# All eight experts' weights resident on chip, addressed by a register

## What is computed

```
logits = x1n @ router_w.T                      # 4096 tokens, 8 experts
top_w, top_i = top_k(softmax(logits), 2)       # two experts per token
h = gelu(x1n @ w1[e])      # w1: 8 x 256 x 1024
y = h @ w2[e]              # w2: 8 x 1024 x 256
out = x1 + sum over the two experts of weight * y
```

## Time and profile before

| what | value |
|---|---|
| median of 3 runs | 728.38 us |
| the three runs | 718.8, 728.38, 732.76 us |
| span of the profiled execution (first to last instruction) | 716.1 us |
| the profiled execution's own time | not listed apart; the runs above lie 2.7 to 16.7 us over its span |
| PE busy | 616.2 us, 86% |
| DVE, ACT, POOL busy | 402.2, 299.7, 256.9 us |
| DMA | 130.52 MB, 182 GB/s mean |

### The profile page before, as it was taken

One profiled execution on the slowest core, in us unless ns is written; L12 is line 12 of the kernel. 1 busy time (PEld: TensorE's weight loads), 2 busy tenths in 40 slices (PEclk: granted clock), 3 DMA queues, 4 the chain that ended last, 5 costly groups with the idle time before them and its releaser, 6 DMA issues.

```text
span 716.1 us, 18339 instructions
## 1 busy us (share of the span) xinstructions
PE 616.2 (86%) x5879; PEld 498.6 (70%) x5879; DVE 402.2 (56%) x1118; ACT 299.7 (42%) x582; POOL 256.9 (36%) x192
## 2 busy tenths in 40 slices
PE   2799988988999830099999999999999999999991
PEld 2578777776887730078787777777787878777880
DVE  1458678687686655045555555555555555555550
ACT  2444634625444200044545444444544454544440
POOL 0213148568475467012133232233231322312322
PEclk9965657557565555599999999999999999999996
DMA  9786486594541425913944938537649358377321
GB/s 313 272 323 224 173 292 223 208 329 176 196 185 75 177 81 178 367 26 54 343 101 102 349 48 260 179 59 222 218 74 369 56 135 298 52 205 243 48 36 22
DMA packets 58964, 130.52 MB, mean 182 GB/s; under 512 B 6384, under 2 KB 38384, under 8 KB 57904
## 3 DMA queue, kind: packets, MB, share of 16 engines
q1 hardware_dynamic: 44384, 110.91, 43.2%
q0 software_dynamic: 13392, 18.10, 14.1%
q10 hardware_dynamic: 1152, 1.07, 0.4%
HBM read 188.49 MB, written 40.13 MB: 319 GB/s over the span
## 4 chain that ended last, share of the span: by engine, by line
PE 69%; DVE 8%; ACT 6%; issue 5%; DMA 5%; POOL 4%; SPq 2%; POOLq 0%; DVEq 0%; ACTq 0%
PE bank L664 16%; PE bank L650 9%; PE bank L652 9%; PE bank L651 9%; PE bank L666 8%; PE bank L542 6%; PE bank L485 5%; DMA out<-ct,dst 2%; PE bank L634 2%; PE bank L527 2%; POOL rows L1282 2%; ACT xn L695 2%; DMA xrow<-rows 1%; POOL hrs L1274 1%; DVE rowb L874 1%
## 5 line engine op out<-in xcount | busy, mean ns | idle before, releaser
L650 PE MATMUL bank<-dt,wring 128*128 128x128 f16 x1136 | 198.5, 220 | 1.1 <-DVE dt L1201 1.1
L652 PE MATMUL bank<-dt,wring 128*128 128x128 f16 x1136 | 198.6, 220 | 0.0
L651 PE MATMUL bank<-dt,wring 128*128 128x128 f16 x1136 | 198.5, 220 | 0.0
L664 PE MATMUL bank<-wring,ct 128*128 128x512 f16 x568 | 192.3, 379 | 1.3 <-DVE ct L1217 1.3
L1217 DVE TENSOR_TENSOR ct<-dt,ct 128x512 f16<-128x512 f32 x142 | 98.3, 692 | 139.0 <-PE bank L666 113.1
L814 ACT ACTIVATE dt<-bank 128x512 f32<-128x512 f32 x142 | 84.8, 597 | 216.3 <-PE bank L652 216.3
L666 PE MATMUL bank<-wring,ct 128*128 128x256 f16 x568 | 154.8, 273 | 0.0
L1318 POOL DMA_INDIRECT out<-ct,dst x48 | 76.6, 1596 | 211.8 <-DMA out<-ct,dst 75.8
L650 PEld LDWEIGHTS bank<-dt,wring 128*128 128x128 f16 x1136 | 111.3, 98 | 25.1 <-issue 15.7
L651 PEld LDWEIGHTS bank<-dt,wring 128*128 128x128 f16 x1136 | 111.4, 98 | 0.9
L652 PEld LDWEIGHTS bank<-dt,wring 128*128 128x128 f16 x1136 | 111.4, 98 | 0.0
(11 more groups left out here) (139 smaller groups left out, 830.2 us busy)
## 6 DMA issues: line engine op xcount, KB each, us to landing
wring<-wsplit SPq DMA_DIRECT2D x284, 512.0 KB
wring<-in_w SPq DMA_DIRECT2D x16, 1024.0 KB, 12.0
xrow<-rows SPq DMA_DIRECT2D x71, 130.0 KB
wsplit<-wring SPq DMA_DIRECT2D x4, 2048.0 KB, 8.4
wsplit<-wcv SPq DMA_DIRECT2D x4, 2048.0 KB, 7.9
xa<-in_x SPq DMA_DIRECT2D x8, 512.0 KB, 9.1
kT<-in_ctx_t SPq DMA_DIRECT2D x8, 512.0 KB, 8.6
ctn<-in_ctx SPq DMA_DIRECT2D x8, 512.0 KB, 8.4
```

The source lines that it names most:

```text
L650: pe.matmul(o, hi, xT[k][:, c, :], start=(c == 0), stop=False)
L651: pe.matmul(o, hi, xT[k][:, CK + c, :], start=False, stop=False)
L652: mm = pe.matmul(o, lo, xT[k][:, c, :], start=False, stop=(c == CK - 1))
L664: pe.matmul(YP[k][:, 0:2 * D], gh[a][:, m4, :], wring[:, k, w:w + 2 * D], start=(a == 0 and m4 == 0), stop=False, skip_group_check=True)
```

## The change

All eight experts' split weights get a place in one tensor `wall` of 128 KB in each partition, at the expert's number. The buffers of the attention stage (`xa`, `kT`, `ctn`) now lie in the places of experts 4 to 7, and the staging buffers of the weight split in those of 0 to 3. A tile's weights are loaded only where its expert differs from that of the tile just before, and SP works five tiles ahead instead of two (with a wait for the stored attention results, since their buffer is overwritten). The place is no longer known when the program is written, so SP's destination and every weight operand of PE is addressed by a register: PE loads the tile's expert from the table, and `weights(e, at, n)` names the slice.

```diff
-        xa = sb("xa", [P, NB, D])
-        kT = [sb(f"kT{p}", [P, G, CK, P]) for p in range(3)]
-        ctn = [sb(f"ctn{p}", [P, G, D]) for p in range(2)]
+        wall = sb("wall", [P, NE, 2 * (W1 + W2)], F16)
+        early = wall[:, NE // 2:NE, :].bitcast(F32).rearrange("p e n -> p (e n)")
+        xa = early[:, 0:NB * D].rearrange("p (b d) -> p b d", d=D)
...
-        wring = sb("wring", [P, RING, 2 * (W1 + W2)], F16)
-        wst = [wring[:, p, :].bitcast(F32) for p in range(2)]
-        wcv1 = sb("wcv1", [P, 2 * (W1 + W2)], F16)
-        wcv = [wring[:, 2, :], wcv1[:, :]]
+        wst = [wall[:, p, :].bitcast(F32) for p in range(2)]
+        wcv = [wall[:, 2 + p, :] for p in range(2)]
...
-            def load_weights(i, k, it):
+            def load_weights(i, o, it):
                 e = sp.value_load(tab[0:1, 0, bass.ds(i, 1)], min_val=0, max_val=NE - 1)
                 need = sp.value_load(tab[0:1, 2, bass.ds(i, 1)], min_val=0, max_val=1)
                 w_e = wsplit[bass.ds(e, 1)].rearrange("o p n -> (o p) n")
+                place = wall[:, bass.ds(e, 1), :].rearrange("p o n -> p (o n)")
                 for half, s_free, s_loaded in ((0, s_h, s_wr1), (1, s_m2, s_wr2)):
-                    after(sp, s_free, 2 * (i - RING + 1))
+                    after(sp, s_free, 2 * (i - OUT + 1))
...
-                        sp.dma_start(wring[:, k, at], w_e[:, at], cond=need).then_inc(s_loaded[k], 16)
+                        sp.dma_start(place[:, at], w_e[:, at], cond=need).then_inc(s_loaded[o], 16)
             def tile(i, k, o, it):
                 load_rows(i, k, it)
-                if not (isinstance(i, int) and i < RING):
-                    load_weights(i, k, it)
+                if not (isinstance(i, int) and i >= TILES - OUT + RING):
+                    j = o + OUT - RING
+                    load_weights(i + OUT - RING, j % OUT, it + j // OUT)
             sp.wait_ge(s_tab, 1)
+            sp.wait_ge(s_x1o, 16 * NG)
...
-                        hi = wring[:, k, c * HID + m * P:c * HID + (m + 1) * P]
-                        lo = wring[:, k, W1 + c * HID + m * P:W1 + c * HID + (m + 1) * P]
+                        hi = weights(e, c * HID + m * P, P)
+                        lo = weights(e, W1 + c * HID + m * P, P)
...
-                    pe.matmul(YP[k][:, 0:2 * D], gh[a][:, m4, :], wring[:, k, w:w + 2 * D],
+                    pe.matmul(YP[k][:, 0:2 * D], gh[a][:, m4, :], weights(e, w, 2 * D),
...
+            def expert(i):
+                return pe.value_load(tab[0:1, 0, bass.ds(i, 1)], min_val=0, max_val=NE - 1)
+            def weights(e, at, n):
+                return wall[:, bass.ds(e, 1), at:at + n].rearrange("p o n -> p (o n)")
             def tile(i, k, o, it):
-                hidden(i, k, it, 0)
+                e = expert(i)
+                hidden(i, k, o, it, e, 0)
                 if not (isinstance(i, int) and i == 0):
-                    output(i - 1, (k - 1) % RING, it, 1)
+                    output(i - 1, (k - 1) % RING, (o - 1) % OUT, it, expert(i - 1), 1)
-                hidden(i, k, it, 1)
+                hidden(i, k, o, it, e, 1)
...
-            link(dve.memset(chg[:, 0:RING], 1.0))
-            link(dve.tensor_tensor(chg[:, RING:TILES], etab[:, RING:TILES], etab[:, 0:TILES - RING], ALU.not_equal))
+            link(dve.memset(chg[:, 0:1], 1.0))
+            link(dve.tensor_tensor(chg[:, 1:TILES], etab[:, 1:TILES], etab[:, 0:TILES - 1], ALU.not_equal))
```

More of the change, by code:

```diff
@@ L116, in build @@
         mhalf = sb("mhalf", [P, R])
-        xa = sb("xa", [P, NB, D])
-        kT = [sb(f"kT{p}", [P, G, CK, P]) for p in range(3)]
-        ctn = [sb(f"ctn{p}", [P, G, D]) for p in range(2)]
+        wall = sb("wall", [P, NE, 2 * (W1 + W2)], F16)
+        early = wall[:, NE // 2:NE, :].bitcast(F32).rearrange("p e n -> p (e n)")
+        xa = early[:, 0:NB * D].rearrange("p (b d) -> p b d", d=D)
+        kT = [early[:, NB * D + p * G * D:NB * D + (p + 1) * G * D].rearrange("p (b j n) -> p b j n", b=G, j=CK)
+              for p in range(3)]
+        ctn = [early[:, NB * D + (3 + p) * G * D:NB * D + (4 + p) * G * D].rearrange("p (b d) -> p b d", b=G)
+               for p in range(2)]
         vt = [sb(f"vt{p}", [P, G, NH, DH + 1]) for p in range(2)]
@@ L306, in build @@
         s_xr = [sem(f"tile_loaded{i}") for i in range(RING)]
-        s_wr1 = [sem(f"tile_first_weights{i}") for i in range(RING)]
-        s_wr2 = [sem(f"tile_second_weights{i}") for i in range(RING)]
+        s_wr1 = [sem(f"tile_first_weights{i}") for i in range(OUT)]
+        s_wr2 = [sem(f"tile_second_weights{i}") for i in range(OUT)]
         s_xtp = sem("tile_transposed")
@@ L337, in spot @@
             def spot(j, it):
-                return OUT * it + j, j % RING, j, OUT // RING * it + j // RING
+                return OUT * it + j, j % RING, j, it
             for j in range(OUT):
@@ L346, in tiles, with it_rows @@
                 tile(*spot(j, TILES // OUT))
+        def it_rows(o, it):
+            return OUT // RING * it + o // RING
         block = stack.enter_context(nc.Block())
@@ L635, in turn, with hidden @@
                 mm.then_inc(s_xtp, 1)
-            def hidden(i, k, it, a):
+            def hidden(i, k, o, it, e, a):
                 if a == 0:
-                    pe.wait_ge(s_wr1[k], 16 * PIECES * (it + 1))
+                    pe.wait_ge(s_wr1[o], 16 * PIECES * (it + 1))
                     pe.wait_ge(s_xtc, i + 1)
@@ L645, in hidden, with output @@
                     m = 4 * a + m4
-                    o = HPS[a][:, m4 * P:(m4 + 1) * P]
+                    h = HPS[a][:, m4 * P:(m4 + 1) * P]
                     for c in range(CK):
-                        hi = wring[:, k, c * HID + m * P:c * HID + (m + 1) * P]
-                        lo = wring[:, k, W1 + c * HID + m * P:W1 + c * HID + (m + 1) * P]
-                        pe.matmul(o, hi, xT[k][:, c, :], start=(c == 0), stop=False)
-                        pe.matmul(o, hi, xT[k][:, CK + c, :], start=False, stop=False)
-                        mm = pe.matmul(o, lo, xT[k][:, c, :], start=False, stop=(c == CK - 1))
+                        hi = weights(e, c * HID + m * P, P)
+                        lo = weights(e, W1 + c * HID + m * P, P)
+                        pe.matmul(h, hi, xT[k][:, c, :], start=(c == 0), stop=False)
+                        pe.matmul(h, hi, xT[k][:, CK + c, :], start=False, stop=False)
+                        mm = pe.matmul(h, lo, xT[k][:, c, :], start=False, stop=(c == CK - 1))
                 mm.then_inc(s_h, 1)
-            def output(i, k, it, a):
+            def output(i, k, o, it, e, a):
                 if a == 0:
-                    pe.wait_ge(s_wr2[k], 16 * PIECES * (it + 1))
+                    pe.wait_ge(s_wr2[o], 16 * PIECES * (it + 1))
                 pe.wait_ge(s_gh, 2 * i + a + 1)
@@ L663, in output @@
                     w = 2 * W1 + (4 * a + m4) * 2 * D
-                    pe.matmul(YP[k][:, 0:2 * D], gh[a][:, m4, :], wring[:, k, w:w + 2 * D],
+                    pe.matmul(YP[k][:, 0:2 * D], gh[a][:, m4, :], weights(e, w, 2 * D),
                               start=(a == 0 and m4 == 0), stop=False, skip_group_check=True)
-                    mm = pe.matmul(YP[k][:, D:2 * D], gl[a][:, m4, :], wring[:, k, w:w + D],
+                    mm = pe.matmul(YP[k][:, D:2 * D], gl[a][:, m4, :], weights(e, w, D),
                                    start=False, stop=(a == 1 and m4 == 3), skip_group_check=True)
                 mm.then_inc(s_m2, 1)
+            def expert(i):
+                return pe.value_load(tab[0:1, 0, bass.ds(i, 1)], min_val=0, max_val=NE - 1)
+            def weights(e, at, n):
+                return wall[:, bass.ds(e, 1), at:at + n].rearrange("p o n -> p (o n)")
             def tile(i, k, o, it):
-                hidden(i, k, it, 0)
+                e = expert(i)
+                hidden(i, k, o, it, e, 0)
                 if not (isinstance(i, int) and i == 0):
-                    output(i - 1, (k - 1) % RING, it, 1)
-                hidden(i, k, it, 1)
+                    output(i - 1, (k - 1) % RING, (o - 1) % OUT, it, expert(i - 1), 1)
+                hidden(i, k, o, it, e, 1)
                 if not (isinstance(i, int) and i == TILES - 1):
-                    turn(i + 1, (k + 1) % RING, it + (k + 1) // RING)
-                output(i, k, it, 0)
+                    turn(i + 1, (k + 1) % RING, it_rows(o + 1, it))
+                output(i, k, o, it, e, 0)
             pe.wait_ge(s_sa, NG)
+            pe.wait_ge(s_tab, 1)
             turn(0, 0, 0)
             tiles(pe, tile)
-            output(TILES - 1, (TILES - 1) % RING, 0, 1)
+            output(TILES - 1, (TILES - 1) % RING, (TILES - 1) % OUT, 0, expert(TILES - 1), 1)
         @block.scalar
```

2 lines of the change are left out of this document (1 added, 1 removed).

## The result

| | before | after |
|---|---|---|
| median of three runs | 728.38 us | 857.34 us (857.19, 857.34, 858.57) |
| ratio after / before | | 1.185 [1.171, 1.199]: slower |
| span of the profiled execution | 716.1 us | 855.3 us |
| a tile (once-a-tile line of DVE) | 5.547 us | 7.586 us |
| table ready | 280.5 us | 289.5 us |

What follows compares the result with a forecast made beforehand. PE's sequencer was to replace PE's matmul stream as bound: 71 x (6.8 - 5.55) = +89 us, with -7.7 at the start and -5.7 at the end, gives a 792 us span, plus 12.3 is 804 us; range 755 to 1180.

Steps and rivals of the forecast that it cites:

- rival A: PE's sequencer: only control instructions cost, the forecast's own case, 804 us, own range 762 to 861; chance 0.50.
- the sum: PE's sequencer time a tile: 10 x 0.10 + 1.3 + 4.0 + 132 x 0.004 = 6.8 us, against 5.55 of matmuls.
- The start: Start of the expert stage: first rows land at 295.2 instead of 302.9, behind fewer weight loads: -7.7 us.
- the end: End of the expert stage: POOL's last scatter catches up with a third of the weight loads: -5.7 us.
- the price of an address: PE's sequencer: 40 fused register operations a tile at 0.10 us each, 4.0 us; bounds 1.3 to 6.3 us.
- Rival C: PE's register work runs beside the queued matmuls, so only the edges count: 715 us, -1.8%; chance 0.14.
- The offset of 12.3 us: Added to the forecast span of 792 us to give the median of the runs, 804 us.
- the first L634 near 295 us: Sign expected in any case at the start of the expert stage: the first L634 comes near 295 us.
- Triples: Sign for A in the hidden layer: matmul triples about 0.2 us apart instead of 0.167.
- Rival B: PE's 64 register-addressed weight loads or matmuls cost 0.032 to 0.10 us each: 946 to 1258 us; chance 0.29.
- Rival D: PE pauses often enough to be granted 1.2 GHz, 11.1 us a tile: about 1110 us; chance 0.07.
- Rival E: Tile order makes weights reload more often, so edges lose some of their 13 us; no chance of its own.

Runs made afterwards that it cites:

- one-slice kernel: Changed kernel with every hidden weight load taking the same slice, still addressed by register (9 address operations a tile instead of 40): one run of 717.14 us beside 726.73.
- fixed-address kernel: Changed kernel with PE back on fixed addresses and without its two register loads a tile: 707.4 us against 730.35 for the kernel before, ratio 0.971.

## Why the prediction was right in its direction and short in its size

**What held.** The time, 857.34 us, lies inside the range of 755 to 1180 and 53 us above the 804 named. The sequencer became the bound (rival A), by the steps named: 40 addresses and two loads a tile, counted in the rows; the clock at 1.00; 33.5 MB less. A load costs 0.63 us (forecast 0.65), or 0.67 in the five tiles of six that lose one. The rest of the tile, 7.586 - 40 x 0.125 - 2 x 0.63 = 1.33 us, stands against 10 x 0.10 + 132 x 0.004 = 1.53 in the sum. The start measured from the table came 8.7 us earlier (forecast 7.7), the end 5.7 (forecast 5.7).

**What was mis-sized: the price of an address.** The sum took 0.10 us, 4.0 us a tile. Eight more of them cost 0.125 each, so 40 cost 5.0: +1.0 us in this term, and with the other terms slightly under, 7.59 instead of 6.8. 71 x 0.79 = 56 us, and that is the miss of 53.3 in time (857.34 - 804) but for small parts. The 0.10 came from two rows of DVE-to-PE handovers, 0.09 for "one more" operation and 0.105 if both share. These values were right, but for other operations: in the changed kernel's expert stage a plain register operation (ALU_OP) is followed 0.093 us later by the next control instruction, a wait 0.105 later, and a fused one 0.100 later. A fused one with weight loads and matmuls behind it is followed 0.124 later. So handing over to the matmuls and back adds about 0.024 us, whether two or four of these instructions lie between. This is the sign of failing that the prediction named itself, that the spacing behind a matmul differs from that between two waits. Both the sum's own bounds (0.032 to 0.158) and A's own range (0.12 each gives 861) held the truth. The duration printed for the operation, 46 ns, is about a third of what it costs.

**Slips in the working.** A's low end doesn't follow from its own words: 50 x 0.09 + 1.3 is 5.8 us a tile, not 6.2. C's condition leaves out the 0.5 us of fixed instructions that the sum has; with them p has to be under 0.075. Neither moves the forecast.

**The offset of 12.3 us** between median and span was taken as constant. After, it is 857.34 - 855.3 = 2.0, and in the repeat of the kernel before 729.94 - 728.1 = 1.8. The other 10 us were the profiled execution's short attention stage. By luck this cancels: the table came 9.0 us later in the profile of after, and 792 + 9.0 + 2.0 + 56 - 1.0 (start) = 858. For the same reason "the first L634 near 295 us" failed as written (L641 after the change, at 303.4) although its mechanism, 22.6 to 13.9 us behind the table, held.

**Triples** were forecast about 0.2 us apart; they are 0.25 in one hidden half and 0.167 in the other. The mean is right and the picture was not: the queue lets the sequencer run ahead over `output`. The plain sum worked because the sequencer of the changed kernel never pauses: from 341 to 810 us its control instructions start at most 0.5 us apart, and more than 0.3 only behind a register load. Where it has time to spare, the sum is too low, as the kernels with 24 and 9 addresses show (5.6, 5.1 and 3.7 us of work at steps of 6.233, 5.804 and 5.714): it stops at the wait for the split rows, and what comes behind that wait starts without a lead.

**Rival B** (the instruction itself slow) is refuted by the spacing in the one-slice kernel and in the changed one: some 8 ns an instruction, as with fixed addresses, where B needed 32 to 100. The Trainium skill (TensorE: Matmul & The Clock Gate, Part 2) gives about 62 ns for a matmul that the firmware has to handle; the trace doesn't show that for a weight load or matmul with a register address. **Rival C** (register work hidden beside the queue) is refuted for this change by the step, but its mechanism exists: two loads vanished at fixed addresses (5.553 to 5.560). The Trainium skill (Advanced Engine Details and Errata, Sequencer Loop) says that other engine instructions can be read and queued while the firmware executes a control instruction. The trace agrees only in part: what was handed over before a load runs on during it, but in the changed kernel the weight loads behind the load of the expert all come after it, the first at 406.17 in the tile shown. C needed an operation under 0.085 us. **Rival D**: the granted clock is 1.00 from 341 to 810 us. **Rival E**: the loads were saved, 97.02 MB moved.

**Open.** Of the 23 us by which the fixed-address kernel is below the kernel before, the stretch behind the table shows 11.5 to 14.4. The rest lies in the attention stage, whose length differs by 15 us between executions, or in the moved buffers. The profiles speak against the buffers: the table is ready between 280.6 and 295.6 us in the eight with moved buffers, and between 280.5 and 295.4 in the five without. No run tests it alone. Nor is it shown why the tile at the head of a turn takes 6.7 us with one load kept in its register: the branch and the second load fit it, but no kernel separates them.

## What to carry to other kernels

Before addressing an operand of a short matmul by a register, count the distinct slices per loop turn, not the instructions: each costs the sequencer an operation of its own, and its work has to stay well below the stream's time, not just under it. Look at what stands behind a wait as well: an address operation there showed in full, though the sequencer had only 3.7 us of work in 5.7. Moving data less often is worth only what transfers cost on the path; here that was the start and the end of the stage, and an order of transfers with fixed addresses got both. Take the price of a sequencer operation from the spacing of starts, since the printed duration leaves out most of it, and time stages from an event of their own where the stage before varies.

## What the runs showed of the hardware that was not expected

- An address operation on PE occupies its sequencer for 0.125 us while its row prints 46 ns, and a load of a register from on-chip memory with its check 0.63 us while TENSOR_LOAD prints 0.30. Without matmuls behind it, a register operation or a wait took 0.09 to 0.105 us.
- A weight load or matmul whose address is in a register passes as fast as a fixed one: L657 to L658 are 0.01 to 0.02 us apart, and 48 instructions of a half are handed over in 0.4 us either way.
- The queue in front of PE let the sequencer get at least 1.98 - 1.33 = 0.65 us ahead while `output` streamed: the hidden half behind it had 1.98 us of address work and still ran at the stream's 1.33.
- Operations behind the sequencer's wait for the split rows are not covered, however little work it has: the first weight load came 0.35 us after the rows with an address to compute, and 0.21 with fixed addresses.
- The attention stage of one and the same kernel took 280.5 us in one execution and 295.4 in another.
